# A graph network's second layer norm: one operation per block with scale and shift, on ScalarE and GpSimd instead of ScalarE and VectorE

## The reference, cut to what matters

```python
def _layernorm(x, axis=-1, eps=1e-05):
    m = jnp.mean(x, axis=axis, keepdims=True)
    v = jnp.var(x, axis=axis, keepdims=True)
    return (x - m) / jnp.sqrt(v + eps)

h = jnp.maximum(_layernorm(x, axis=-1), 0.0)
x = x + _L0_gnn_ref(h, edge_index, edge_attr_128, ...)   # 2 layers: segment_sum(relu(h[src] + edge_attr), dst), MLP with batch norm
h = jnp.maximum(_layernorm(x, axis=-1), 0.0)             # the second layer norm: the change is here
x = x + _L1_gnn_ref(h, edge_index, ...)                  # 2 layers: segment_sum(h[src], dst), MLP
```

## Time and profile before

| | us |
|---|---|
| median of 3 runs | 2753.68 |
| lowest and highest | 2751.79, 2753.81 |
| the profiled execution | 2753.93 |
| its span in the profile | 2752.1 |
| PE busy | 1908.3 (69%) |
| DVE busy | 1701.1 (62%) |
| ACT busy | 735.4 (27%) |
| POOL busy | 1941.4 (71%) |

### The profile page before, as it was taken

The page is one execution under the profiler, slowest core; times in us unless marked ns, Lnnn a source line. Parts: engine busy times, 40 slices in busy tenths (PEclk is TensorE's granted clock), DMA queues, the critical chain, the costliest instruction groups (busy, mean ns, idle before and its releaser), DMA issues.

```text
span 2752.1 us, 35065 instructions
## 1 busy us (share of the span) xinstructions
PE 1908.3 (69%) x9399; PEld 1278.4 (46%) x9399; DVE 1701.1 (62%) x2880; ACT 735.4 (27%) x1002; POOL 1941.4 (71%) x2048
## 2 busy tenths in 40 slices
PE   2476656566656672666566666656578999989999
PEld 2354444344444442435444444434444566546555
DVE  7797677777777764777777777777774221342212
ACT  4132222222222251333333333333361000210001
POOL 6777777777777727777777777777707777377773
PEclk8687777787888786878878888888878999999999
DMA  6343433343434333444444444444426566465653
GB/s 199 97 144 107 129 107 122 113 128 114 135 114 136 120 112 98 132 138 127 149 128 149 135 156 141 156 149 149 146 92 203 190 219 198 135 208 186 211 193 101
DMA packets 228544, 396.82 MB, mean 144 GB/s; under 512 B 43080, under 2 KB 133020, under 8 KB 228388
## 3 DMA queue, kind: packets, MB, share of 16 engines
q0 software_dynamic: 65024, 133.30, 18.1%
q1 hardware_dynamic: 111684, 162.15, 17.2%
q10 hardware_dynamic: 51680, 99.63, 10.4%
HBM read 333.10 MB, written 61.81 MB: 143 GB/s over the span
## 4 chain that ended last, share of the span: by engine, by line
POOL 52%; PE 22%; issue 18%; DVE 4%; DMA 3%; ACT 1%; DVEq 1%; POOLq 0%; SPq 0%; ACTq 0%
POOL xg L675 50%; PE psA L1537 14%; PE psG L1552 4%; POOL xg L695 2%; DMA xg<-node_table,src_all 2%; PE psG L1601 2%; PE psA L1609 1%; DVE xp_room L1131 0%; DVE hid L1077 0%; PE psG L1631 0%; DVE acc L1030 0%; DVE hid L1247 0%; PE psA L1618 0%; DVE xp_room L955 0%; DVEq L1052 0%
## 5 line engine op out<-in xcount | busy, mean ns | idle before, releaser
L675 POOL DMA_INDIRECT xg<-node_table,src_all x1520 | 1437.3, 946 | 506.9 <-issue 458.3
L1510 PE MATMUL psG<-hid,xp_room 128*128 128x160 f32 x3072 | 614.2, 376 | 421.6 <-DVE hid L1077 411.7
L1510 PEld LDWEIGHTS psG<-hid,xp_room 128*128 128x128 f32 x3072 | 595.3, 255 | 466.3 <-issue 455.8
L1494 PE MATMUL psA<-cell_room,xp_room 128*128 128x512 f16 (+1 forms) x2336 | 551.6, 388 | 299.2 <-ACT count_out L742 253.3
L1117 DVE TENSOR_SCALAR cell_room<-psG,cell_all 128x932 f16<-128x932 int16 x1088 | 684.6, 688 | 0.0
L695 POOL DMA_INDIRECT xg<-node_table,idx x480 | 468.1, 975 | 250.6 <-issue 248.7
L759 ACT COPY psG<-xp_room 128x512 f32<-128x512 f32 x384 | 226.5, 590 | 1257.7 <-DVE xp_room L1131 1226.5
L1494 PEld LDWEIGHTS psA<-cell_room,xp_room 128*128 128x128 f16 x2336 | 230.7, 103 | 582.7 <-ACT count_out L742 287.8
L1131 DVE TENSOR_TENSOR xp_room<-psG,xg 128x512 f32<-128x512 f32 x380 | 257.3, 677 | 385.8 <-DMA xg<-node_table,src_all 372.2
L1030 DVE TENSOR_TENSOR acc<-acc,row_slot 128x38 f32 x192 | 38.7, 202 | 385.3 <-ACT row_slot L838 360.7
L1077 DVE SCALAR_TENSOR_TENSOR hid<-loc_all,round_off,psG 128x2560 f32<-128x2560 f32 x96 | 274.7, 2862 | 0.1
(11 more groups left out here) (156 smaller groups left out, 804.5 us busy)
## 6 DMA issues: line engine op xcount, KB each, us to landing
xp_room<-in_edge_attr_dram ACTq DMA_DIRECT2D x95, 768.0 KB
cell_room<-count_store SPq DMA_DIRECT2D x16, 2850.0 KB
count_store<-count_out SPq DMA_DIRECT2D x96, 465.5 KB
hid<-count_store SPq DMA_DIRECT2D x16, 2736.0 KB
xg<-node_table,src_all POOLq DMA_INDIRECT x1520
xp_room<-in_edge_attr_dram ACTq DMA_DIRECT2D x95, 256.0 KB
row_slot<-node_table SPq DMA_DIRECT2D x1024, 0.5 KB
hid<-node_table SPq DMA_DIRECT2D x1024, 0.5 KB
```

The lines of the kernel that those rows point to most:

```text
L675: nc.gpsimd.indirect_dma_start(xg[:, n % XG, u, j, :], None, x if n < RAW_TURNS else table, bass.IndirectOffsetOnAxis(ap=src_all[:, s, j:j ...
L1494: last = nc.tensor.matmul(psA[:, bank, 0:w], src_hot[:, hots(n) % 2, at, :], cells[:, c % CELL_RING, c0:c0 + w], start=first, stop=end)
L1510: last = nc.tensor.matmul(psG[:, q, h * WIN:(h + 1) * WIN], ea[:, t, u, j, :], rows[:, u, j, :], start=(u == slots[0] and j == 0), stop=(u ...
```

## The change

Only the second layer norm changes; the first keeps its form. DVE now also forms `ln_shift` = -mean/std. ACT writes relu(x * rstd + shift) for the 36 blocks of groups 0 to 8, in one instruction per block with two per-partition operands. POOL does groups 9 to 12: per block x * rstd + shift, and then one max(.., 0) per group. DVE keeps only the scaling of the turned columns. SP and PE wait for `rows_ready` (ACT's groups) or `rows_normed` (POOL's), still in order of g. After its 36 blocks ACT waits for POOL's four groups and raises `rows_ready` by four for the later readers.

```diff
@@ def store_table(version) on SP; turn_rows(q) on PE has the same choice with q == 1
-                    sp.wait_ge(rows_ready, version * LG + g + 1)
+                    if version == 2 and g >= BY_ACT_ROWS:
+                        sp.wait_ge(rows_normed, g - BY_ACT_ROWS + 1)
+                    else:
+                        sp.wait_ge(rows_ready, version * LG + g + 1)
@@ POOL, between the gathers of layer 1 and load_rounds
+            pool.wait_ge(ln_ready, 1)
+            for g in range(BY_ACT_ROWS, GROUPS):
+                b0, nb = g * GB, len(group_blocks(g))
+                for b in group_blocks(g):
+                    last = nc.gpsimd.tensor_scalar(rows_h[:, b, :], rows_x[:, b, :], ln_rstd[:, b:b + 1], ln_shift[:, b:b + 1],
+                                                   ALU.mult, ALU.add)
+                last.then_inc(rows_shifted, 1)
+                pool.wait_ge(rows_shifted, g - BY_ACT_ROWS + 1)
+                nc.gpsimd.tensor_scalar(rows_h[:, b0:b0 + nb, :], rows_h[:, b0:b0 + nb, :], 0.0, None, ALU.max
+                                        ).then_inc(rows_normed, 1)
@@ ACT, norm_rows(q, version), for q == 1
+                    act.wait_ge(ln_ready, 1)
+                    for g in range(BY_ACT_ROWS):
+                        for b in group_blocks(g):
+                            last = act.activation(rows_h[:, b, :], rows_x[:, b, :], ACT.Relu, bias=ln_shift[:, b:b + 1],
+                                                  scale=ln_rstd[:, b:b + 1])
+                        last.then_inc(rows_ready, 1)
+                    act.wait_ge(rows_ready, 2 * LG + BY_ACT_ROWS)
+                    for g in range(BY_ACT_ROWS, GROUPS):
+                        act.wait_ge(rows_normed, g - BY_ACT_ROWS + 1)
+                        act.sem_inc(rows_ready, 1)
@@ DVE, norm_rows(q)
                 link(nc.vector.reciprocal(ln_rstd[:, :], ln_rstd[:, :]))
+                if q == 1:
+                    nc.vector.tensor_tensor(ln_shift[:, :], ln_neg_mean[:, :], ln_rstd[:, :], ALU.mult).then_inc(ln_ready, 1)
                 for g in range(GROUPS + LAG):
-                    if g < GROUPS:
+                    if q == 0 and g < GROUPS:
```

More of the change, by code:

```diff
@@ L300, in gnn_kernel @@
         ln_rstd = sb("ln_rstd", [P, BLOCKS])
+        ln_shift = sb("ln_shift", [P, BLOCKS])
         bn_stats = sb("bn_stats", [P, GROUPS, 6])
@@ L385, in gnn_kernel @@
         centred = sem("centred")
+        ln_ready = sem("ln_ready")
+        rows_shifted = sem("rows_shifted")
+        rows_normed = sem("rows_normed")
         bias_added = sem("bias_added")
@@ L451, in gnn_kernel @@
         PARAMS = 16 * (2 * 6 + 4 + 3 + 1 + 2)
-        CENTRED = (GROUPS - 4, GROUPS)
+        CENTRED = GROUPS - 4
+        BY_ACT_ROWS = GROUPS - 4
         LAG = 2
@@ L720, in norm_rows @@
                     act.wait_ge(table_written, 16 * LG * version)
[L721 to L724, removed]
+                if q == 0:
+                    for g in range(CENTRED):
+                        for b in group_blocks(g):
+                            last = act.activation(rows_h[:, b, :], rows_x[:, b, :], ACT.Relu, bias=ln_neg_mean[:, b:b + 1])
+                        last.then_inc(centred, 1)
+                else:
+                    act.wait_ge(ln_ready, 1)
+                    for g in range(BY_ACT_ROWS):
+                        for b in group_blocks(g):
+                            last = act.activation(rows_h[:, b, :], rows_x[:, b, :], ACT.Relu, bias=ln_shift[:, b:b + 1],
[5 more added lines that the diff above has]
+                        act.sem_inc(rows_ready, 1)
             def centre_raw(n):
@@ L970, in norm_rows @@
                                                in1=ln_var[:, :], op0=ALU.mult, op1=ALU.add).then_inc(ln_var_ready, 1)
[L971 to L976, removed]
+                if q == 0:
+                    for g in range(CENTRED, GROUPS):
+                        for b in group_blocks(g):
+                            last = nc.vector.tensor_scalar(rows_h[:, b, :], rows_x[:, b, :], ln_neg_mean[:, b:b + 1], 0.0,
+                                                           ALU.add, ALU.max)
+                        if g == GROUPS - 1:
+                            link(last)
                 dve.wait_ge(ln_std_ready, q + 1)
                 link(nc.vector.reciprocal(ln_rstd[:, :], ln_rstd[:, :]))
+                if q == 1:
+                    nc.vector.tensor_tensor(ln_shift[:, :], ln_neg_mean[:, :], ln_rstd[:, :], ALU.mult).then_inc(ln_ready, 1)
                 for g in range(GROUPS + LAG):
-                    if g < GROUPS:
+                    if q == 0 and g < GROUPS:
                         b0, nb = g * GB, len(group_blocks(g))
-                        if g < CENTRED[q]:
-                            dve.wait_ge(centred, q * CENTRED[0] + g + 1)
+                        if g < CENTRED:
+                            dve.wait_ge(centred, g + 1)
                         nc.vector.tensor_tensor(rows_h[:, b0:b0 + nb, :], rows_h[:, b0:b0 + nb, :],
@@ L1469, in turn_rows @@
                 for g in range(GROUPS):
-                    pe.wait_ge(rows_ready, (0, 2)[q] * LG + g + 1)
+                    if q == 1 and g >= BY_ACT_ROWS:
+                        pe.wait_ge(rows_normed, g - BY_ACT_ROWS + 1)
+                    else:
+                        pe.wait_ge(rows_ready, (0, 2)[q] * LG + g + 1)
                     if g >= 4:
```

## The result

The changed kernel takes 2776.2 us (median of six runs, 2775.9 to 2781.3), the kernel before 2752.5 (six runs). The ratio is 1.0085, with a 95% interval of [1.0075, 1.0096]. It is slower by 0.85%, where 2755.0 was forecast. The profiled execution took 2776.8 us, its span is 2774.8, 22.7 longer than before.

A forecast was written before the change was run, and what follows sets the result against it. DVE was taken to set the norm's pace; of two branches, 1.15 and 1.35 us late, the later counts: +1.3 us, the rest costing or gaining nothing, so 2755.0 against the median, range 2751.3 to 2758.8.

The forecast's parts named there:

- POOL's 13 blocks and 4 maxima: Second norm: POOL's new work beside ACT takes 7.3 us, done by 2055.3, far ahead of ACT.
- Start and blocks of ACT: Second norm: ACT starts 0.9 us later, at 2047.88; blocks 0.385 us apart, group 8 written at 2061.83.
- rival A: Second norm, ACT: second operand free in a stream of blocks; 2.0 us gained, 2751.7 us; chance 0.12.
- The upper bound: POOL's 17 norm instructions each priced as an indirect gather: 21.3 us, done at 2069.2.
- Rival B: Second norm: POOL finishes late and decides; 2758.1 us at 17 us of work, 2762.4 at 21.3; chance 0.12.
- PE and DVE: Second norm: PE's transposes burst behind group 8 at clock 0.50; DVE free at 2066.50, 1.15 us late.
- ACT ahead of the split: Second norm: ACT's loads, index copies and first quarter wait for finished rows, ending 2066.7, 1.35 us late; this branch decides.
- Table and gathers: Stores 8 to 12 go together, so layer 2's gathers start 2.0 us later, at 2068.2, at no cost.
- The slack of 1.2 us at the end of layer 2: PE needs the last gather 1.2 us after it is ready, so a 0.15 us delay of POOL fits.
- the signs that the prediction is wrong: ACT's blocks 0.3 us apart, POOL's last maximum behind ACT's last block, or PE waiting for gathers in layer 2.
- rival C: Gathers decide: five stores together run slower than 285 GB/s or land later; 2756.3 with 2.5 us more; chance 0.09.

The follow-up runs named there:

- the run with maxima alone: The kernel before with only the 4 maxima added on a scratch tile behind layer 1's gathers, no scale-and-shift; 2773.8 us beside 2753.76.
- the version above: Second norm without arithmetic on POOL: DVE makes groups 1, 4, 7, 10, ACT the nine others, its loads unwaited; 2755.62 us beside 2758.6 for the kernel before.

## Why the prediction was wrong

The step that failed is "POOL's 13 blocks and 4 maxima". It priced them by their own time in the norm, 7.3 us beside ACT's blocks, and the sum took the 2000 gathers of POOL outside the norm as unchanged. The sum thus had no term for the length of a gather. The runs show that this is the term that counts: in the norm POOL is done before ACT, while the block of maxima with its waits makes each gather 11 ns longer, also those ahead of it. That is 17.55 us ahead of the norm. Of the 3.1 us behind it the share of the gathers isn't shown. The run with maxima alone has 1.83 and 1.12 there, but among the thirteen kernels with 944 or 947 ns layer 2 lasts from 341.04 to 342.51 us and layer 3 from 343.77 to 347.70, and the changed kernel's 342.06 and 347.78 lie in that spread or 0.1 beside it.

The steps within the norm:

- *Start and blocks of ACT.* ACT starts 1.43 us behind the last variance step, forecast 1.41, and 36 blocks take 13.96, forecast 13.95. The second operand costs 0.093 us in a stream as alone (0.385 from start to start, where it was 0.292); rival A falls. The Trainium skill, page "ScalarE: Activation LUTs", section "What ACT_TABLE_LOAD costs", states some 93 ns for each pointer operand and an overlap of neighbours of some 93 ns; the trace agrees with both.
- *POOL.* It took 10.95 us instead of 7.3, by 2076.41, 3.0 ahead of ACT's end. A scale-and-shift of a block is 0.444 us, and a maximum of 512 columns 1.5, that is 2.9 ns a column where iota had suggested 0.97. The sentence that every computing row of POOL is near 1 ns a column was a wrong reading: the select of a 128x128 tile, 0.282 us, is 2.2 a column. (The upper bound, 17 x 1.246, is 21.2 and not 21.3.) Rival B forecast a slower kernel, but by another mechanism: POOL wasn't late in the norm.
- *PE and DVE.* PE's granted clock stays 0.50 in the burst, the 1.2 GHz level. DVE is free at 2084.18, which is 2066.63 without the 17.55, forecast 2066.50.
- *ACT ahead of the split.* This branch decides, with 2.06 where the sum had 1.35. The rows are those of the chain of waits after (start us, us, what), and answer to the earlier trace rows:

```profile
2079.81 0.29 ACTq L477
...
2080.37 0.64 ACTq L478
...
2081.92 0.15 ACTq L479
...
2082.10 0.02 ACTq L479
...
2083.02 0.20 ACT idx L851
2083.22 1.59 ACT xp_room L884
```

  And from the timeline of ACT:

```profile
2083.02 0.20 ACT L851 COPY idx<-src_all 128x16 int32 x1 [0.21 <-issue]
2083.13 3.15 ACT L884 ACTIVATE xp_room<-rows_h,use_counts 128x1664 bf16<-128x1664 f32 x2
```

  Waits and hand-ons of `rows_normed` take 0.40 us from 2079.41 on (forecast 0.1), the loads 2.31 (2.25) to 2082.12, and from there to the start of the first quarter, 2083.13, it is 1.01 (0.70), of which the last copy of indices waits 0.21 for its issue. These three make 0.67 of the 0.7.
- *Table and gathers.* The first gather of layer 2 starts at 2085.90, or 2068.35 without the 17.55, forecast 2068.2. The slack of 1.2 us at the end of layer 2 didn't hold, since gathers run through from gather 33 on and some 200 of them are 11 ns longer each, 2.2 us (an estimate). PE now waits for a gather there; in the run without maxima, whose gathers have 944 ns, it doesn't:

```profile
2393.78 2.44 PE L1588 MATMUL psG<-rows_h,xg 128*128 128x160 f32 x16 [0.83 <-DMA xg<-node_table,idx]
```

  This was listed among the signs that the prediction is wrong. It is rival C's wait, though not for C's reason.

How far the sum was off within the norm can be read from the run that leaves out the maxima: its norm takes 20.97 us, 2.09 more than before, where 1.3 was forecast. Its whole time, 2756.1 us, lies in the range, but 2.5 below the kernel before in its job, so the whole time says nothing on 1 or 2 us. The range didn't hold the change, because no case in it let a gather itself become longer.

## What stays open

What in the chip makes a gather longer isn't shown. The median is the same for the gathers ahead of the added instructions and behind them, so it isn't something that an instruction leaves behind for the gathers that follow it in the program. The step of 11 ns goes with what POOL's program holds behind layer 1's gathers; that is how the twenty kernels sort. Whether the maximum as an operation or POOL's waits for its own semaphore count, no run separates: 13 scale-and-shifts with such a wait behind each would. Nor was it tried whether two or three maxima behind the gathers give a value between 944 and 955. The step of 3 ns is open altogether, since no program was profiled in two jobs.

## What to carry to other kernels

Before you move work to an engine, look at what that engine issues over and over and what share of the chain it holds: 50% of this kernel's chain were GpSimd's gathers, so 11 ns on each (1.2%) cost 17.5 us in layers 0 and 1, where the best norm found here wins 2.3. After such a move, first compare the median duration of the engine's other instructions, also of those that run ahead of the edited place. If POOL issues the critical gathers, look first for idle time on DVE for elementwise work, as the version above does. Not all arithmetic on POOL did harm here, but the length of the gathers has to be read again after each addition.

## What the runs showed of the hardware

- The length of an indirect gather of 128 rows on GpSimd has nearly one value through a profiled execution: 944, 947, 955 or 958 ns (median), with the shortest up to 6 ns below. Four or more maxima, with GpSimd's waits between them, behind the gathers of layer 1 raised it by 11 ns, 13 multiplications with additions there didn't (944). One kernel without arithmetic on GpSimd had 947.
- Elementwise fp32 work on GpSimd: 128x128 with two pointers 0.444 us and 128x7 0.343, which is 0.83 ns for each further column; a maximum of 128x128 0.52 and of 128x512 1.49, 2.5 ns for each. The select of 128x128 took 0.282, a fill of 128x512 0.52 to 0.55.
- PE's granted clock rose to 1.00 in the version without arithmetic on POOL, from 2059.5 to 2065.0, after 0.50 from 2053 to 2058. The windows of that version (us, PE, PEld, DVE, ACT, POOL busy, PEclk, DMA share, GB/s):

```profile
2053.00:2058.00 5.00, 4.37 (x19) 3.97 (x20) 4.83 (x14) 5.00 (x14) 0.00 (x0) 0.50 0.67 195
2059.50:2065.00 5.50, 3.61 (x25) 2.67 (x25) 5.46 (x13) 5.37 (x16) 0.00 (x0) 1.00 0.88 255
```

  The changed kernel stayed at 0.50 in its burst:

```profile
2079.40:2083.40 4.00, 3.89 (x17) 3.49 (x17) 2.90 (x5) 0.79 (x5) 0.00 (x0) 0.50 0.83 242
```
